# A cross-attention and mixture-of-experts layer on one core: batch 3's projections among batch 0's scores, weights held back, and a third accumulator

## The reference

```python
qp = layernorm(x) @ Wq.T                    # 16 heads of 16
k, v = split(ctx @ Wkv_expand.T, 2)         # causal: only the first 256 of 512 keys count
attn = softmax(where(causal, q k^T / 4, min))
x = x + (attn @ v) @ Wout.T
h = layernorm(x)
w, i = top_k(softmax(h @ gate_w.T), 4)      # w divided by its sum
y[tok] += w * (silu(h[tok] @ w_gate[e]) * (h[tok] @ w_up[e])) @ w_down[e]   # at most 128 tokens for an expert
x = x + y + (silu(h @ sw_gate) * (h @ sw_up)) @ sw_down
```

## Time and profile before

| | us |
|---|---|
| median of the runs | 219.53 |
| runs | 214.23, 219.53, 221.49 |
| the profiled execution | 214.88 |
| its span, first to last instruction | 213.1 |
| TensorE busy (modelled) | 185.3 |
| VectorE busy | 128.1 |
| Pool busy | 96.3 |
| ScalarE busy | 80.8 |

### The profile page before, as it was taken

One profiled execution on the slowest core, in us unless ns is written; L12 is line 12 of the kernel. 1 busy time (PEld: TensorE's weight loads), 2 busy tenths in 40 slices (PEclk: granted clock), 3 DMA queues, 4 the chain that ended last, 5 costly groups with the idle time before them and its releaser, 6 DMA issues.

```text
span 213.1 us, 3899 instructions
## 1 busy us (share of the span) xinstructions
PE 185.3 (87%) x1369; PEld 137.5 (65%) x1369; DVE 128.1 (60%) x360; ACT 80.8 (38%) x173; POOL 96.3 (45%) x128
## 2 busy tenths in 40 slices
PE   7884785889798999899968898995999999999980
PEld 2663442767675777568836686783878887676860
DVE  2774696736479845993484546868655553354054
ACT  3583230647355524761296313412123323333000
POOL 7822499862285401530064000034477878867100
PEclk9999999999999999999999999999969999999996
DMA  6789999999559503010861038962044445545865
GB/s 179 203 128 130 132 127 131 126 235 312 179 155 330 136 19 121 3 49 8 240 219 49 3 104 282 310 206 74 28 75 59 78 88 85 82 68 64 213 205 197
DMA packets 22459, 28.94 MB, mean 136 GB/s; under 512 B 2457, under 2 KB 17801, under 8 KB 22441
## 3 DMA queue, kind: packets, MB, share of 16 engines
q1 hardware_dynamic: 18944, 23.06, 45.7%
q0 software_dynamic: 3184, 5.38, 13.2%
q10 hardware_dynamic: 313, 0.27, 0.4%
HBM read 15.91 MB, written 6.42 MB: 105 GB/s over the span
## 4 chain that ended last, share of the span: by engine, by line
PE 40%; DVE 17%; POOL 15%; DMA 13%; issue 9%; ACT 2%; SPq 2%; ACTq 1%; DVEq 0%; POOLq 0%
PE s_ps L1430 7%; DMA odd_d<-y_rows,tok_i 6%; PE m_ps L1446 4%; PE o_ps L1350 4%; DVE top L878 3%; PE m_ps L1388 3%; POOL out L602 3%; PE m_ps L1504 3%; DMA k_rows<-k_parts 2%; DMA xn_t<-odd_d 2%; POOL odd_d L602 2%; PE s_ps L1536 2%; DMA wkv<-in_wkv_t 2%; PE m_ps L1274 2%; PE t_ps L1334 2%
## 5 line engine op out<-in xcount | busy, mean ns | idle before, releaser
L535 POOL TENSOR_SCALAR_AFFINE_SELECT probs<-probs 128x256 f32<-128x256 f32 (+1 forms) x48 | 22.9, 489 | 39.0 <-ACT probs L662 37.8
L878 DVE TENSOR_REDUCE top<-s_ps 128x2 f32<-128x512 f32 (+1 forms) x48 | 32.3, 687 | 7.1 <-PE s_ps L1300 6.4
L662 ACT ACTIVATE probs<-t_ps 128x512 f32<-128x512 f32 x48 | 27.9, 597 | 10.0 <-PE t_ps L1334 6.4
L1430 PE MATMUL s_ps<-xn_t,sgu 128*128 128x256 f32 (+1 forms) x96 | 23.5, 385 | 0.0
L1334 PE MATMUL t_ps<-q_rows,k_rows 128*128 128x256 bf16 (+1 forms) x128 | 19.6, 247 | 1.8 <-ACT probs L662 1.1
L1430 PEld LDWEIGHTS s_ps<-xn_t,sgu 128*128 128x128 f32 (+1 forms) x96 | 16.5, 181 | 3.4 <-issue 0.6
L1297 PE MATMUL s_ps<-mask_b,ident_b 128*128 128x256 bf16 (+1 forms) x48 | 15.0, 312 | 4.2 <-DVE top L878 3.7
L1300 PE MATMUL s_ps<-k_rows,q_rows 128*128 128x128 bf16 (+1 forms) x128 | 18.3, 246 | 0.0
L590 POOL DMA_INDIRECT xn<-xn_d,tok_i x4 | 4.2, 1062 | 25.3 <-DVE tok_i L1053 24.4
L726 ACT ACTIVATE xg_t<-t_ps 128x256 f32<-128x256 f32 x16 | 6.2, 385 | 23.8 <-PE t_ps L1524 23.1
L1334 PEld LDWEIGHTS t_ps<-q_rows,k_rows 128*128 128x128 bf16 x128 | 10.3, 98 | 5.7 <-ACT probs L662 2.6
(11 more groups left out here) (186 smaller groups left out, 390.0 us busy)
## 6 DMA issues: line engine op xcount, KB each, us to landing
k_rows<-k_parts SPq DMA_DIRECT2D x24, 128.0 KB, 6.3
q_rows<-q_parts SPq DMA_DIRECT2D x24, 128.0 KB, 7.5
k_rows<-in_w_dn SPq DMA_DIRECT2D x12, 176.0 KB
out<-xs SPq DMA_DIRECT2D x8, 256.0 KB, 2.4
wgu_early<-in_w_gu SPq DMA_DIRECT2D x4, 352.0 KB
q_rows<-in_w_gu SPq DMA_DIRECT2D x4, 352.0 KB
v_ones<-in_w_gu SPq DMA_DIRECT2D x4, 352.0 KB
probs<-in_w_gu SPq DMA_DIRECT2D x4, 352.0 KB
```

The costliest lines, as they stand in the source:

```text
L535: nc.gpsimd.affine_select(out=v, in_=v, compare_op=ALU.is_ge, fill=0.0, base=0, pattern=[[0, v.shape[1]], [1, P]], channel_multiplier=-1). ...
L662: t_ring.emptied(nc.scalar.activation(probs[:, g % 2, u, :], t_ring.bank(job)[:], ACT.Exp, scale=HD ** -0.5), job)
L878: s_ring.emptied(nc.vector.tensor_reduce(dst, src, AX.X, ALU.max), job)
L1430: last = nc.tensor.matmul(s_ring.bank(("gu", b, c))[0:size, S * half:S * half + S], sgu[:, hc, half, at:at + size], xn2_t[:, hc, S * b:S * ...
```

## The change

- Batch 3's `x`, `k`, `v`, `q` move from batch 0's tail to the front: `x` 3 ahead of batch 0's score units, `v` 3 among them, `k` 3 and `q` 3 behind them. Batch 0's tail gets the first four score units of batch 2, and the other eight are spread over batch 1's twelve places (`BESIDE`). `q` 2 gets the bank of `o_ring`. ScalarE's and VectorE's orders follow; batch 3's two splits stand in batch 0's stage.
- Pool: the large memsets stand between the last parts, batch 2's last q part and batch 3's stand behind masks of batch 0, the further constants behind masks of batch 1, and the clearing DMAs and one iota behind masks of batch 2. The idle products before `shift` 0 are gone.
- SyncE: the shared weights wait for batch 1's shift, and the first expert weights for batch 2's.
- Three accumulators instead of two (`out`, `second_d`, `third_d`), experts in turn. The third is loaded first and added by Pool, the second by VectorE as the odd one was.

The diff, cut to its core:

```diff
+ACCS = 3
...
+EARLY_UNITS = 4
+BESIDE = [[[u] for u in range(3 * NG)] for b in range(B)]
+for _i in range(3 * NG):
+    BESIDE[1][_i] = [u for u in range(EARLY_UNITS, 3 * NG)
+                     if (u - EARLY_UNITS) * 3 * NG // (3 * NG - EARLY_UNITS) == _i]
+
 TAIL_FILL = (
-    ((("x", 3), ("k", 3)), (("v", 3),), (("q", 3),), (), ()),
+    ((("s", 2, 0),), (("s", 2, 1),), (("s", 2, 2),), (("s", 2, 3),), ()),
...
-KEEP_BUSY = {("k", 0): 9, ("q", 0): 3, ("x", 1): 2, ("s", 0, 0): 4, ("shift", 0): 7}
+KEEP_BUSY = {("k", 0): 9, ("q", 0): 3, ("x", 1): 2, ("s", 0, 0): 4}
...
-                  ("k", 2), ("x", 2), ("q", 2)])
+                  ("k", 2), ("x", 2), ("q", 2), ("x", 3), ("v", 2)])
     for u in range(3 * NG):
         steps.append(("s", 0, u))
         if u == 4:
-            steps.append(("v", 2))
-    steps.append(("shift", 0))
+            steps.append(("v", 3))
+    steps.extend([("k", 3), ("q", 3), ("shift", 0)])
     for b in range(B):
         for g in range(NG):
             for u in range(3):
                 steps.append(("st", b, g, u))
                 if b + 1 < B:
-                    steps.append(("s", b + 1, 3 * g + u))
+                    steps.extend(("s", b + 1, v) for v in BESIDE[b][3 * g + u])
...
+OTHER_RING = {("q", 2): "o"}
...
-        odd_rows = reuse(xn2_t, P, NT, H)
+        second_rows = reuse(xn2_t, P, NT, H)
+        third_rows = reuse(wgu_early, P, NT, H)
...
             sp.dma_start(gate[:], gate_t.rearrange("(c p) n -> p c n", p=P)).then_inc(gate_in, 16)
+            after_shift(1)
             sp.dma_start(sgu[:], sw_gu.rearrange("(c p) g i -> p c g i", p=P)).then_inc(sw_in, 16)
             sp.dma_start(sdn[:, 0:2, :], sw_dn[0:2 * P].rearrange("(c p) n -> p c n", p=P)).then_inc(sw_in, 16)
             sp.dma_start(sdn[0:IS - 2 * P, 2, :], sw_dn[2 * P:IS]).then_inc(sw_in, 16)
 
-            for e in group(0):
-                load_gate_up(e)
-                load_down(e)
             send_rows(3)
             store_normalised(0)
             t_ring.wait(sp, ("st", 1, NG - 1, 2))
             after_shift(2)
+            for e in group(0):
+                load_gate_up(e)
+                load_down(e)
             for e in group(1):
                 load_down(e)
             store_normalised(1)
...
-            for n, (acc, dst) in enumerate(((out, xs), (odd_d, odd_rows))):
-                sp.wait_ge(scattered[n], 16 * ((E - LATE) // 2))
+            for n, acc, dst, done in ((2, third_d, third_rows, third_in), (0, out, xs, out_in),
+                                      (1, second_d, second_rows, second_in)):
+                sp.wait_ge(scattered[n], 16 * len(range(n, E - LATE, ACCS)))
                 for i in range(2):
                     rows, tiles = slice(T // 2 * i, T // 2 * i + T // 2), slice(NT // 2 * i, NT // 2 * i + NT // 2)
-                    sp.dma_start(dst[:, tiles], acc[rows].rearrange("(t p) c -> p t c", p=P)).then_inc(sums_in[i], 16)
+                    sp.dma_start(dst[:, tiles], acc[rows].rearrange("(t p) c -> p t c", p=P)).then_inc(done[i], 16)
...
+            def last_part(k, b):
+                n = "kq".index(k)
+                pool.wait_ge(mid_ready, 2 * b + n + 1)
+                if b == 1:
+
+                    pool.wait_ge(low_ready, 2)
+                if b >= 2:
+                    pool.wait_ge(rows_in[k][b - 2], SENT)
+                nc.gpsimd.tensor_tensor(parts[k][:, b % 2, 2, :], rest[:, n, :], parts[k][:, b % 2, 1, :],
+                                        ALU.subtract).then_inc(low_ready, 1)
+                pool.wait_ge(low_ready, 2 * b + n + 1)
...
-            last_parts(1)
-            last_parts(2)
+            last_part("k", 1)
             link(nc.gpsimd.memset(v_ones[:, :, :, :, HD:], 1.0))
+            last_part("q", 1)
             pad_rows(q_rows, 1, ROW_BUFS, 0.0)
+            last_part("k", 2)
             pad_rows(k_rows, 1, ROW_BUFS, ONE_PAIR)
             constant(nc.gpsimd.memset(zero_rows[:], 0.0))
...
             for b in range(B):
-                if b == 1:
-
-                    last_parts(3)
-                    pool.dma_start(xn2_d[T:T + CAP], zero_rows[:]).then_inc(zeros_stored, 16)
-                    pool.dma_start(out[T:T + CAP], zero_rows[:]).then_inc(zeros_stored, 16)
-                    pool.dma_start(odd_d.rearrange("(t p) c -> p t c", p=P),
-                                   zero_rows[:].unsqueeze(1).to_broadcast([P, (T + CAP) // P, H])).then_inc(zeros_stored, 16)
-                if b == 2:
-
-                    constant(nc.gpsimd.iota(token_iota, pattern=[[1, T]], base=0, channel_multiplier=0,
-                                            allow_small_or_imprecise_dtypes=True))
                 for g in range(NG):
                     causal(b, g)
+                    pool.wait_ge(probs_masked, 3 * (NG * b + g + 1))
+                    if (b, g) == (0, 0):
+                        last_part("q", 2)
+                    if (b, g) == (0, 1):
+                        last_part("k", 3)
+                    if (b, g) == (0, 2):
+                        last_part("q", 3)
+                    if (b, g) == (1, 0):
+                        link(nc.gpsimd.memset(cst[:], 1.0))
+                        link(nc.gpsimd.affine_select(out=cst[:], in_=cst[:], compare_op=ALU.is_gt, fill=0.0,
+                                                     base=0, pattern=[[1, P]], channel_multiplier=-1))
+                        link(nc.gpsimd.tensor_copy(above_b[:], cst[:]))
...
+                    if (b, g) == (1, 3):
+                        link(nc.gpsimd.memset(cst[:], 1.0))
+                        link(nc.gpsimd.tensor_copy(tok_vals[:, :, :, 2], v))
+                        link(nc.gpsimd.memset(key[:], MARK))
+                        constant(nc.gpsimd.memset(four[:], MARK))
+                    if (b, g) == (2, 0):
+                        pool.dma_start(xn2_d[T:T + CAP], zero_rows[:]).then_inc(zeros_stored, 16)
+                        pool.dma_start(out[T:T + CAP], zero_rows[:]).then_inc(zeros_stored, 16)
+                        for acc in (second_d, third_d):
+                            pool.dma_start(acc.rearrange("(t p) c -> p t c", p=P),
+                                           zero_rows[:].unsqueeze(1).to_broadcast([P, (T + CAP) // P, H])).then_inc(zeros_stored, 16)
+                    if (b, g) == (2, 1):
+                        constant(nc.gpsimd.iota(token_iota, pattern=[[1, T]], base=0, channel_multiplier=0,
+                                                allow_small_or_imprecise_dtypes=True))
...
-                if e >= 2:
-
-                    pool.wait_ge(scattered[e % 2], 16 * (e // 2))
+                if e >= ACCS:
+
+                    pool.wait_ge(scattered[e % ACCS], 16 * (e // ACCS))
...
+            for b in range(B):
+                pool.wait_ge(third_in[b // 2], 16)
+                pool.wait_ge(out_in[b // 2], 16)
+                v = slice(QT * b, QT * b + QT)
+                nc.gpsimd.tensor_tensor(xs[:, v], xs[:, v], third_rows[:, v], ALU.add).then_inc(third_added, 1)
+                pool.wait_ge(third_added, b + 1)
...
             copy_x(2)
             normalise(3)
+            copy_k(2)
+            copy_x(3)
+            copy_v(2)
             copy_q(2)
-            copy_v(2)
+            copy_v(3)
             load_table(ACT.Exp)
+            copy_k(3)
             send_shift(0)
+            copy_q(3)
...
+            def add_second(b):
                 v = slice(QT * b, QT * b + QT)
-                dve.wait_ge(sums_in[b // 2], 32)
-                chained(nc.vector.tensor_tensor(xs[:, v], xs[:, v], odd_rows[:, v], ALU.add))
+                dve.wait_ge(third_added, b + 1)
+                dve.wait_ge(second_in[b // 2], 16)
+                chained(nc.vector.tensor_tensor(xs[:, v], xs[:, v], second_rows[:, v], ALU.add))
...
             stats_of(3)
+            scale_of(3)
             split(1, 1, "q")
             split(2, 0, "k")
-            scale_of(3)
-            split(2, 1, "q")
             for u in range(NS):
                 maxima(0, u)
             shift_parts(0)
+            split(2, 1, "q")
...
-                            maxima(b + 1, 3 * g + u)
+                            for v in BESIDE[b][3 * g + u]:
+                                maxima(b + 1, v)
...
+                    if b == 0 and g == 0:
+                        split(3, 0, "k")
+                    if b == 0 and g == 1:
+                        split(3, 1, "q")
```

More of the change, by code:

```diff
@@ L560, in _ @@
-            link(nc.gpsimd.tensor_copy(tok_vals[:, :, :, 0], v))
-            link(nc.gpsimd.iota(v, pattern=[[P, NT], [0, E]], base=-T, channel_multiplier=0,
-                                allow_small_or_imprecise_dtypes=True))
-            link(nc.gpsimd.tensor_copy(tok_vals[:, :, :, 1], v))
-            link(nc.gpsimd.memset(cst[:], 1.0))
-            link(nc.gpsimd.tensor_copy(tok_vals[:, :, :, 2], v))
-            link(nc.gpsimd.memset(key[:], MARK))
-            constant(nc.gpsimd.memset(four[:], MARK))
```

(10 more changed lines are left out.)

81 lines of the change are left out of this document (40 added, 41 removed).

## The result

The changed kernel is slower. Its median is 222.56 us (222.29 to 224.69, 5 runs) against 218.25 us (214.23 to 221.49, 5 runs) for the kernel before; the ratio is 1.033 (95% interval 1.028 to 1.037). The profiled execution took 224.69 us, with a span of 222.6 us and a mean granted clock of 0.945, against 214.88, 213.1 and 0.984. The four other executions of the changed kernel took 222.3 to 222.9 us, so some 2 us of what follows belong to the profiled one.

The account below looks back on a forecast made before the run. It took TensorE to bound the expert loop and VectorE batch 1's stage. Terms 1.0 + 0.7 + 2.9 + 1.2 - 0.3 - 0.7 = 4.8 us took 214.88 to 210.1 us; median forecast 211.5, range 206 to 217.

Parts of the forecast that it names:

- The start: From the start to batch 0's first `st`: shift transposes at 34.9 instead of 35.91; gain 1.0 us, bounds 0 and 1.7.
- Batch 0's stage and tail: Batch 0's mask wait gone, less a TensorE stall: gain 0.7 us; tail about 7.15 us against 10.09: gain 2.9.
- the rival with late rows (C): Batch 3's rows come too late for its first score unit: 3.9 us slower than before, 218.8 us; chance 0.08.
- Batch 1's stage: Eight units instead of twelve, 2.4 us, less 0.9 waiting for Pool's masks and 0.3 for held VectorE operations: gain 1.2.
- rival B: Pool is the new bound in batch 1's and 2's stages, masks later than counted: 2.9 us saved, 212.0; chance 0.14.
- Batch 2's stage: Pool's four clearing DMA issues, 3.5 us, delay group 1's masks and the iota: loss 0.3 us, bounds 0 and 1.
- The end: Last scatter issued 1.5 us earlier, but 3 MB loaded and Pool's four adds: loss 0.7 us; bounds gain 1.5, loss 2.7.
- rival A: At the end, adds in turns and the third load's traffic on the scatters lose 2.7 us: 212.1; chance 0.16.
- three signs of being wrong: Batch 1's stage starting after 57.5, batch 2's first unit waiting for DMA, last add over 2 us later after last `down`.

## Why the prediction was wrong

I predicted 210.1 us on the profiled scale, and it was 224.69 (for the median 211.5, range 206 to 217, and it was 222.56). What failed are three costs and a term that wasn't there: Pool's holding of VectorE's small operations (0.3 us charged, 1.4 measured without the clock), the clearing DMAs, priced only as time in Pool's queue (0.3 charged for the stage, 3.3 measured, clock included), the end, where I priced the third load but not what it does to the last scatter (0.7 charged, 3.48 measured), and the clock, at nothing. The 14.6 us between forecast and measurement, term by term:

- **The start** (gain 1.0): 0.42 lost in the profiled execution, a miss of 1.4. Its first projections took twice as long as those of the same code in the kernel with the third loaded last, though the granted clock shows 1.00 in both:

```profile
5.83 2.05 PE L1292 MATMUL m_ps<-lat,wkv 128*128 128x256 f32 x4 [0.68 <-DMA wkv<-in_wkv_t]
```

```profile
5.82 1.10 PE L1292 MATMUL m_ps<-lat,wkv 128*128 128x256 f32 x4 [0.67 <-DMA wkv<-in_wkv_t]
```

There the shift is at 34.42, where I had put it at 34.9. Four of the eleven traces with the new order have this faster start, with the shift at 34.25 to 34.84, and seven the slower one, with 36.11 to 37.48; with the old order it is two (35.72, 35.91) against one (38.19). So the step holds where the first products are not slow. Whether the new order makes the slow start likelier, no run tells.

- **Batch 0's stage and tail** (gain 0.7 + 2.9 = 3.6): 2.86 gained. The wait for batch 0's masks is gone, the first unit of batch 1's stage starts at 58.12 against 60.77 with no wait for the shift (56.20 in the trace with the faster start, where my terms put it at 56.2), and the rival with late rows (C) didn't occur: SyncE has issued the last of them by 65.4. That this tail needs the weights held back was right too: without that it costs 2.03 us.
- **Batch 1's stage** (gain 1.2): 1.36 lost. With Pool's constants elsewhere the gain is 22.74 - 21.17 = 1.57, where I had 2.4 without charges. The step that failed is my 0.3 us for "Pool's casts of up to 1 us will also hold some of VectorE's small operations". I had the row at 21.10 and asked which single operations it would hit, not what stands behind them: a maximum, and behind it TensorE. Pool's block costs 2.9. The trace of the kernel with the third loaded last has this block in a run where the clock stayed at 1.00 there: 22.56 us. So the holding costs 22.56 - 21.17 = 1.4 us, and the clock that fell behind it 24.10 - 22.56 = 1.5. The wait of `o_ps` for Pool's masks, for which I had charged 0.9 (and the sum behind it, 9.4 + 1.9, is 11.3 and not 11.6, so it should have been 1.2), isn't in the trace; rival B had the right engine and the wrong way.
- **Batch 2's stage** (loss 0.3): 3.30 lost. I costed the clearing DMAs only as time in Pool's queue, in front of masks. That issuing them holds VectorE was in no term, though the rows at 33.49 showed a memset doing it for 1.5 us. With the clearing moved the stage costs what it did before (23.10 against 23.06). With one issue less, in the kernel with two accumulators, the held operation took 0.77 us and not 1.77, the clock stayed at 1.00 there, and the stage took 24.44.
- **Batch 3's stage** (nothing): 3.96 lost, in a stage where nothing was edited. At full clock it takes 20.24 (two accumulators), 0.8 more than before: TensorE waits 1.86 us for the normalised rows, not 1.06. In the trace with two accumulators VectorE comes to the last step of the norm 0.5 us later and needs 1.05 us for it, not 0.73; that this is because the chain meets Pool's masks in another phase is what I suppose, and no run moved them. The other 3.2 us are the clock, half from 116 to 123 us behind that wait. With two accumulators the same wait of 1.86 us was followed by a clock of 1.00, so the fall does not always follow; in the five other kernels of the table with the new order this stage took 21.67 to 23.40.
- **The end** (loss 0.7, bound 2.7): 3.48 lost. I had costed when each load ends, from a load of 1 MB in 4 us, and had not asked what a load does to the scatter that the last load waits for: 2.6 us (7.34 less 4.77). The turns of Pool and VectorE, part of my rival A, are real: 1.84 us a pair, and 4.63 us for VectorE's four adds. The Trainium skill, "SBUF — State Buffer", section "SBUF: two separate sides", says that a Pool operation that reads SBUF and a VectorE operation with two SBUF inputs exclude each other for a whole instruction. The trace agrees, with the turns above. They are the smaller part, 2.0 us against the scatter's 2.6; the last scatter's earlier issue, for which I had 1.5, gave 1.3 back.

The clock was in no term of the sum. Taken together, the half clock of the profiled execution costs, in the stages of batches 1 and 3, 1.5 + 3.2 us, and I estimate about 1 in batch 2's (0.43 of 4 us is 1.7, less what VectorE would have held anyway). Over a third of the miss is that, and half with the 1.9 us of the slow first products. The rows of the kernel before, with windows at 1.00, gave no price for it. I had seen its mean of 0.984 and taken it for granted.

Two of my three signs of being wrong came: batch 1's stage started at 58.12, later than 57.5, and the last add ended 3.5 us later after the last `down` than before. A chance of 0.08 for slower was far too low. Of my rivals, A and B point at the places of 8.1 of the 12.1 us lost (batch 1's and 2's stages and the end), and neither has the size; batch 3's 4.0 us are in no rival. I gave each as a small deduction from the forecast, never both with the work behind them.

## What to carry to other kernels

Pool's queue isn't only judged by when its own results are wanted. Every long operation or DMA issue of Pool, put beside a chain of small VectorE operations, is charged to that chain and to all that stands behind it; put it into a stretch where VectorE has no such chain, and price it as if VectorE did it. A second buffer that lets a transfer start earlier has to be charged with what it then runs beside, above all with the last transfer of the chain that sets the end.

## What the runs showed of the hardware

- **Issuing a DMA from Pool holds VectorE.** Two issues of 1.04 and 1.02 us held a VectorE operation on 128x2 for 1.77 us, until the second was over. With one issue less it took 0.77 us, with those issues elsewhere 0.28.
- **A scatter that adds lands later beside a load.** From the issue of the last scatter to that of the load waiting for it: 3.82 us with one load begun 2.0 us behind it; 4.5 to 5.4 us with one begun 1.1 to 1.4 us behind it (five traces); 6.35 us with one begun 0.5 us behind it (one trace); 7.25 to 8.1 us with a load in the same moment and another 2 us later (seven traces). In these traces the scatter lands later the sooner a load begins behind it.
- **The granted clock falls for several us behind a stall.** Behind windows of 4 us in which TensorE was busy 1.79, 1.70 and 1.67 us, the granted clock fell to 0.5 (1.2 GHz) for stretches of 3.3 to 7 us. But it also fell behind 9.86 busy of 10 us, and it stayed at 1.00 behind two such windows without idle products: one with 1.67 us busy (two accumulators, batch 3's stage) and one with 1.89 (third loaded last, batch 1's stage). What decides stays open; a stall can cost about as much again in clock as it costs in waiting (1.4 and 1.5 us in batch 1's stage).
- **A 24 KB DMA beside weight loads** was waited for until 7.45 us after its issue, and had landed within 2.8 us without them.
